# First attention of a two-layer transformer kernel: value products by a table of chunks, maxima of two banks taken at once, no repeated products

## What is computed

```python
q = layer_norm(qkv[:, :, 0], q_gamma, q_beta)
k = layer_norm(qkv[:, :, 1], k_gamma, k_beta)
v = qkv[:, :, 2]
q, k = apply_rope(q, k)
attn = jnp.einsum('bqhd,bkhd->bhqk', q * D ** -0.5, k)      # 16 heads of 16
attn = jax.nn.softmax(attn, axis=-1)
out = jnp.einsum('bhqk,bkhd->bqhd', attn, v).reshape(B, S, C)
out = jnp.einsum('bsc,oc->bso', out, w_proj) + b_proj
```

## Time and profile before

| | |
|---|---|
| median of three runs | 1911.12 us (1906.89 to 1915.96) |
| the profiled execution | 1908.63 us, of it 1906.6 us span of instructions |
| first maximum take of the first attention | 133.0 us from the span's start |
| last transpose of maxima (L867) | 767.9 us |
| last maximum take (L1000) | 764.4 us |
| granted PE clock over the span | 0.968 of full speed |

### The profile page before, as it was taken

The page is one execution under the profiler, slowest core; times in us unless marked ns, Lnnn a source line. Parts: engine busy times, 40 slices in busy tenths (PEclk is TensorE's granted clock), DMA queues, the critical chain, the costliest instruction groups (busy, mean ns, idle before and its releaser), DMA issues. The chain is left out here.

```text
span 1906.6 us, 34780 instructions
## 1 busy us (share of the span) xinstructions
PE 1798.0 (94%) x12778; PEld 1176.0 (62%) x12778; DVE 1430.6 (75%) x2814; ACT 1116.5 (59%) x2212; POOL 529.8 (28%) x686
## 2 busy tenths in 40 slices
PE   8989999999999999799999989999999987999995
PEld 4545444444444444388888875555555566999994
DVE  7879999999999999367677656567666454766665
ACT  4645888888888888622333215455463632655555
POOL 5760000233000001032223212212425243544444
PEclk9976999999999999899999999999999998999998
DMA  4883734565434512023444256545565324565555
GB/s 170 279 261 50 127 74 101 128 145 124 87 57 70 80 33 86 18 78 111 153 143 148 89 189 139 142 99 145 145 155 152 111 78 152 151 152 144 144 114 199
DMA packets 146599, 239.18 MB, mean 125 GB/s; under 512 B 25829, under 2 KB 81158, under 8 KB 146448
## 3 DMA queue, kind: packets, MB, share of 16 engines
q1 hardware_dynamic: 113312, 171.48, 36.7%
q0 software_dynamic: 17024, 34.25, 7.0%
q10 hardware_dynamic: 16112, 31.46, 4.5%
HBM read 137.49 MB, written 96.60 MB: 123 GB/s over the span
## 5 line engine op out<-in xcount | busy, mean ns | idle before, releaser
L1000 DVE TENSOR_REDUCE b_mx<-b_PM 128x1 f32<-128x512 f32 x1024 | 621.3, 682 | 18.5 <-PE b_PM L854 18.1
L976 ACT ACTIVATE b_probs<-b_PS 128x512 f32<-128x512 f32 x1000 | 524.1, 607 | 69.2 <-PE b_PS L908 53.6
L854 PE MATMUL b_PM<-b_kst,b_qst 48*128 48x512 f32 x888 | 281.8, 431 | 0.0
L2929 ACT ACTIVATE d_probs<-d_PS 128x512 f32<-128x512 f32 (+3 forms) x384 | 166.0, 497 | 183.4 <-PE d_PS L2830 167.5
L908 PE MATMUL b_PS<-b_qst,b_kst 50*128 50x512 f32 x744 | 257.2, 437 | 1.8
L2968 DVE TENSOR_REDUCE d_mx<-d_PM 128x2 f32<-128x1024 f32 (+1 forms) x192 | 179.5, 950 | 92.4 <-PE d_PM L2782 50.8
L908 PEld LDWEIGHTS b_PS<-b_qst,b_kst 50*128 50x128 f32 x744 | 120.4, 184 | 163.6 <-ACT b_probs L976 148.1
L2884 POOL TENSOR_SCALAR_AFFINE_SELECT d_probs<-d_probs 128x128 f32<-128x128 f32 x256 | 74.1, 303 | 265.6 <-ACT d_probs L2929 260.7
L796 POOL CAST b_mhalves<-b_maxima 128x16 fp32r<-128x16 f32 x32 | 6.3, 196 | 506.8 <-DVE b_maxima L1009 506.8
L854 PEld LDWEIGHTS b_PM<-b_kst,b_qst 48*128 48x128 f32 x888 | 142.1, 185 | 5.3
L880 PE MATMUL b_PO<-b_probs,x_v 128*32 128x384 f32 (+2 forms) x2048 | 145.2, 390 | 0.0
(11 more groups left out here) (322 smaller groups left out, 3751.2 us busy)
## 6 DMA issues: line engine op xcount, KB each, us to landing
halves<-a_parts SPq DMA_DIRECT2D x7, 2048.0 KB, 8.7
qk<-c_halves ACTq DMA_DIRECT2D x7, 2048.0 KB
w_w<-L_ffn_fc1T SPq DMA_DIRECT2D x12, 1024.0 KB, 5.0
w_w<-L_ffn_fc2T SPq DMA_DIRECT2D x12, 1024.0 KB
b_qst<-halves SPq DMA_DIRECT2D x72, 128.0 KB, 4.3
b_kst<-halves SPq DMA_DIRECT2D x72, 128.0 KB, 7.2
d_qst<-qk SPq DMA_DIRECT2D x36, 256.0 KB, 5.1
d_kst<-qk SPq DMA_DIRECT2D x36, 256.0 KB, 7.3
```

Source lines behind the costliest of these rows:

```text
L854: mm = pe.matmul(PM[n % MBANKS][:], qst[buf][at, p, first:first + P], kst[buf][at, p, kh * BLK:(kh + 1) * BLK], start=True, stop=True)
L976: act.activation(probs[:, s % RING], score_bank(g, s)[:], ACT.Exp).then_inc(exped, 1)
L1000: dve.tensor_reduce(mx[:, half, (r * PAIRS0 + p) * TPH + t, kh:kh + 1], PM[n % MBANKS][:], AX.X, ALU.max)\
L2929: act.activation(probs[:, s % RING, 0:w], PS[bank(s)][:, 0:w], ACT.Exp).then_inc(exped, 1)
```

## The change

- `REPEATS` is emptied: each maximum product is issued once.
- The bursts are gone. After each unit PE issues the value products that the table `CHUNKS` names for it: an entry is (unit of the half after whose products it comes, round, first quarter, end quarter). An entry of 32 or more falls in the next half. An entry covers one round, and there are 13 per half in 12 places. The transpose stays behind the units 22 and 54.
- The output is copied after the units 41 and 9 (before: 36 and 4).
- `PM` becomes one tensor of four banks, and `mx` is set to -3e38 once. For the steps in `WHOLE_STEPS`, 12 of 32 in a group, and all 24 steps that are made ahead of the first group, the DVE waits for both products, takes the maximum over both banks (1024 elements) in one instruction, and raises `max_taken` by 2 when it is done. The second column of `mx` keeps -3e38 there.
- In the last group, the rounds from unit 23 on begin with one round more of values.

```diff
-    LAG, BREAK = 6, 3
-    REPEATS = {7: 3, 8: 2, 9: 2, 10: 2}
...
+    REPEATS = {}
+
+    CHUNKS = [(12, 0, 0, 3), (15, 0, 3, 4), (16, 1, 0, 3), (19, 1, 3, 4), (19, 2, 0, 2), (22, 2, 2, 4),
+              (25, 3, 0, 2), (27, 3, 2, 4), (30, 4, 0, 4), (33, 5, 0, 4), (36, 6, 0, 2), (38, 6, 2, 4),
+              (41, 7, 0, 4)]
+
+    def values_after(s):
+
+        found = []
+        for half in range(HALVES):
+            for at, R, first, end in CHUNKS:
+                at += half * UNITS // HALVES
+                if at % UNITS == s:
+                    found.append((-(at // UNITS), half * TPB + R, first, end))
+        return sorted(found)
...
+    COPY_UNITS = [41, 9]
+    WHOLE_STEPS = [2, 4, 6, 11, 13, 15, 18, 20, 22, 27, 29, 31]
+
+    def whole(n):
+
+        n -= AHEAD * HALVES
+        return n < 0 or n % UNITS // HALVES in WHOLE_STEPS
...
-        PM = [a.ps(f"PM{i}", [P, BLK]) for i in range(MBANKS)]
+        PM = a.ps("PM", [P, MBANKS, BLK])
...
-            def burst(g, k):
-                for s in units_of(k):
-                    score(g, s)
-                for i, at in enumerate(TURN_PLACES):
-                    u = HALVES * g + 1 + i
-                    if at // SBANKS == k and u < TURNS:
-
-                        pe.wait_ge(exped, g * UNITS + exps_before(at - SBANKS + 1) + SBANKS)
-                        turn_max(u)
-                for before, R, first, end in values_after(k):
+            def unit(g, s):
+                score(g, s)
+                if s + 1 in TURN_UNITS and (u := HALVES * g + 1 + TURN_UNITS.index(s + 1)) < TURNS:
+
+                    pe.wait_ge(exped, g * UNITS + exps_before(TURN_PLACES[TURN_UNITS.index(s + 1)] - SBANKS + 1) + SBANKS)
+                    turn_max(u)
+                for before, R, first, end in values_after(s):
                     if g + before >= 0:
                         values(g + before, R, first, end)
...
-            s, v = WIDE_FROM, quarters_through(WIDE_BURST - 1)
-            for R in range(WIDE_FROM // G0 + 1, ROUNDS + 2):
+            s, v = WIDE_FROM, quarters_until(WIDE_FROM)
+            for R in range(v // G0 + 2, ROUNDS + 2):
...
+            dve.memset(mx[:], -3.0e38).then_inc(mx_set, 1)
+            dve.wait_ge(mx_set, 1)
...
-                dve.wait_ge(max_scores, n + 1)
-                dve.tensor_reduce(mx[:, half, (r * PAIRS0 + p) * TPH + t, kh:kh + 1], PM[n % MBANKS][:], AX.X, ALU.max)\
-                   .then_inc(max_taken, 1)
+                out = mx[:, half, (r * PAIRS0 + p) * TPH + t]
+                if not whole(n):
+                    dve.wait_ge(max_scores, n + 1)
+                    dve.tensor_reduce(out[:, kh:kh + 1], PM[:, n % MBANKS], AX.X, ALU.max).then_inc(max_taken, 1)
+                elif kh == 0:
+                    dve.wait_ge(max_scores, n + HALVES)
+                    both = PM[:, n % MBANKS:n % MBANKS + HALVES].rearrange("p h n -> p (h n)")
+                    dve.tensor_reduce(out[:, 0:1], both, AX.X, ALU.max).then_inc(max_taken, HALVES)
```

More of the change, by code:

```diff
@@ L630, in exps_before, with quarters_until @@
         return sum(place(s) < at for s in range(UNITS)) - sum(place(s) - LAPS >= at for s in range(UNITS))
-    LAG, BREAK = 6, 3
-    REPEATS = {7: 3, 8: 2, 9: 2, 10: 2}
-    def quarters_through(k):
-        last = units_of(k)[-1] if k >= 0 else -1
-        def due(v):
-            w = v % (UNITS // HALVES)
-            return last >= v + LAG + max(0, BREAK - w // G0)
-        return sum(due(v) for v in range(-UNITS, UNITS)) - UNITS
-    def values_after(k):
-        v, end, found = quarters_through(k - 1), quarters_through(k), []
-        while v < end:
-            stop = min(end, v // G0 * G0 + G0)
-            found.append((v // UNITS, v % UNITS // G0, v % G0, (stop - 1) % G0 + 1))
-            v = stop
-        return found
-    def copied_after(half):
-        end = UNITS // HALVES if half == 0 else 0
-        k = min(k for k in range(BURSTS) if quarters_through(k) >= end)
-        return units_of(k)[-1] - 1
-    COPY_UNITS = [copied_after(half) for half in range(HALVES)]
+    REPEATS = {}
[10 more added lines that the diff above has]
+        return sorted(found)
+    def quarters_until(s):
+        return sum(end - first for half in range(HALVES) for at, R, first, end in CHUNKS if at + half * UNITS // HALVES < s)
+    assert all(at >= R * G0 + G0 - 1 for at, R, first, end in CHUNKS)
+    COPY_UNITS = [41, 9]
[3 more added lines that the diff above has]
+        return n < 0 or n % UNITS // HALVES in WHOLE_STEPS
     def step_at(x):
@@ L853, in max_product @@
                 for _ in range(times):
-                    mm = pe.matmul(PM[n % MBANKS][:], qst[buf][at, p, first:first + P],
+                    mm = pe.matmul(PM[:, n % MBANKS], qst[buf][at, p, first:first + P],
                                    kst[buf][at, p, kh * BLK:(kh + 1) * BLK], start=True, stop=True)
@@ L938, in _ @@
             for g in range(GROUPS):
-                for k in range(BURSTS if g < GROUPS - 1 else WIDE_BURST):
-                    burst(g, k)
-            s, v = WIDE_FROM, quarters_through(WIDE_BURST - 1)
-            for R in range(WIDE_FROM // G0 + 1, ROUNDS + 2):
+                for s in range(UNITS if g < GROUPS - 1 else WIDE_FROM):
+                    unit(g, s)
+            s, v = WIDE_FROM, quarters_until(WIDE_FROM)
+            for R in range(v // G0 + 2, ROUNDS + 2):
                 while s < min((R + 1) * G0, UNITS):
```

15 lines of the change are left out of this document (6 added, 9 removed).

## The result

Four runs of the changed kernel took 1971.77 us in the median (1967.34 to 1976.85), the kernel before beside them 1910.03 (1906.89 to 1915.96): a ratio of **1.0333** (95% interval 1.0306 to 1.0361), 61.7 us more. The forecast was 1949, the range ended at 1964. One remark for all comparisons: layer 1, which no kernel here changes, differs by up to 18 us between profiled executions, so that small differences are read within the attention.

A forecast was written before the change was run, and what follows sets the result against it. The DVE was taken to bound the first attention, PE just behind. Terms: +0.4 and +38.3 from +1.32 a half over 29 halves, +2.0 lead, -1.5 cold start: +39 on 1908.63, forecast 1949 us, range 1925 to 1964.

The forecast's parts named there:

- 12/13 to 22/23: Stretch of a half between the merged takes of these units: 6.47 us forecast, of which 0.46 DVE idle.
- Two products behind one wait. This decides: Merged takes await both products, free banks together; work between three pairs per half idles the DVE: +1.32 us a half.
- pairs 20, 21, 22 and the transpose: Step of PE's work before merged take 22/23, costed at 0.34 + 0.24 + 1.16 us.
- ACT doesn't interfere: ACT's exps and copies in a half need about 17 of 21 us, so they were taken not to delay anything.
- 0.57 from product 13 to its take: Delay from the second product of split pair 12/13 to the merged take's start; also used at 22/23 and 30/31.
- 12 x 0.17 = +2.0: Lead of 24 merged steps at half clock: 2.56 us per merged pair against 2.39 single; bounds -1.3 and +4.
- I take -1.5: Group 0's cold start: fewer repeated products and quarters before the clock rises save 1.5 us; bounds -4 and +2.
- The last group's rest is paced by exps and stays: End of the attention, rest of the last group: no change in time, forecast 0.
- They cover idle time, so I cost their removal at nothing: Five repeated products per half, units 7 to 10: they fill PE's idle time, so removing them costs nothing at full clock.
- Rival 1: Faster: DVE has 0.33 us less a half, no new waits; half 18.90 us, whole 1886 us; chance 8%.
- Rival 2: Slower by less: only two direct stops count; half 20.3 us, whole 1929 us; chance 12%.
- rival 3: Clock falls without the repeated products: one slow stretch every four groups adds some 15 us, 1964 us; chance 5%.

The follow-up runs named there:

- e1: Changed kernel with every take single, in the lead too; table and single products stay: 19.25 us a half, median 1905.39 us, ratio 0.9963.
- e6: Table of chunks with single takes, lead included, plus merged takes at units 24/25 and 28/29 of each half: 19.15 us a half, 1902.46 us, ratio 0.9944.
- e7: Table of chunks with single takes, lead included, plus merged takes at 12/13 and 30/31, split by values: 20.06 us a half, 1926.92 us, ratio 1.0075.
- e9: Changed kernel with the values of units 22 and 54 issued before the transpose, not behind it: 21.22 us a half, 1965.29 us, ratio 1.0267.
- e13 to e16: One chip, in order: changed kernel again 1969.13 us; it with single lead 1980.59; table with single takes but merged lead 1905.55; table alone again 1903.91.
- e8: Table with single takes, merges at 24/25 and 28/29, last group's first output copied after unit 36 instead of 41: 19.15 us a half, 1899.32 us, ratio 0.9923.
- e10: Table with single takes, lead included, and the repeated products back in units 7 to 10 of each half: 19.64 us a half, 1919.34 us, ratio 1.0029.
- e12: Kernel before with only the repeated products removed; bursts and single takes stay: 20.09 us a half, 1926.70 us, ratio 1.0083.
- e16: Second run of the table with all takes single, lead included, and no repeated products: 1903.91 us.
- e4: Kernel before with the merged takes alone, lead included; bursts, repeats and output copies as before: 20.76 us a half, 1948.92 us, ratio 1.0178.

## Why the prediction was right and wrong

The forecast was 23 us too low. The mechanism, two products behind one wait, held; what failed are the size of one of its pieces (12/13 to 22/23), the cold start and the last group.

- **The bound and the rhythm: right.** The DVE set the pace and PE was just behind. Its need of 19.23 us a half is what e1 takes, with no idle time at all.
- **"Two products behind one wait. This decides": right in kind, and within 0.08 us in four of five pieces.** All four are at or above the forecast. From 8/9 to 12/13 I had 3.04 (3.12 in the timeline above), 26/27 to 30/31 3.26 (3.32), 22/23 to 26/27 2.34 (2.34), 30/31 to 8/9 5.87 (mean of the halves 5.87). e6 and e7 show the cause by itself, for the pairs that values split.
- **The piece from 12/13 to 22/23 failed: 6.47 forecast, 6.88 in the timeline.** By its own steps: product 16 came 0.14, not 0.05, after the take (525.20 against 523.83 + 1.23); the transpose came 0.29 later than the step "pairs 20, 21, 22 and the transpose" had it; the way from product to merged take was 0.64, not 0.57. The middle one is the largest. I took the transpose's 1.16 from the earlier trace rows, where three scores stand in a burst whose exps are long done. In the table unit 22 comes 0.24 behind unit 21, and the transpose writes into a `PS` bank that waits for an exp. "ACT doesn't interfere" compared sums (17 of 21 us), and the wait is one of order. e9 takes it away and gives back 0.27.
- **"0.57 from product 13 to its take" was mis-sized:** 0.63 at all three split pairs. The 0.57 of the earlier trace rows is a take of one bank, and e7, where 22/23 isn't merged, still has it there (0.57) beside 0.63 at its two merged pairs. Three times 0.06 are 0.2 a half. Why a take of two banks starts 0.06 later was not tried.
- Together these make 0.5 us a half: 21.49 instead of 20.98, and over 28 halves 14.6 of the 25 us between the 39 of the sum and the 64 that the last exp came later. The rest is 1.2 in the lead, 4.3 to take 22, 2.4 in the next piece and 2.4 at the end.
- **"12 x 0.17 = +2.0" for the lead: 3.2 measured,** inside its bounds.
- **"I take -1.5" for the cold start: the wrong sign.** To take 22 of group 0 it is +2.8, and the next piece is 2.4 more than forecast. I counted what PE has less to do before the clock rises and took the moment of the rise as given; it came later (granted clock 0.52 from 160 to 192 us, against 0.77 before). Only partly explained, see e13 to e16.
- **"The last group's rest is paced by exps and stays": wrong by 2.4.** I didn't follow `COPY_UNITS` into the last group, where the order of exps, not the DVE, decides when `PO` is free: 1.3 us of pause, and 1.2 by the clock that fell with it (e8).
- **"They cover idle time, so I cost their removal at nothing": wrong in both directions.** In the table the repeats would have cost 0.39 a half (e10); in the bursts they hold up the clock (e12, +0.8%). In this change as a whole these don't show, since the table keeps the clock without them.
- **The saving of 0.055 per merge: right** (0.06 in e6). The Trainium skill ("VectorE: DVE Perf Modes", the cycle table of the TRN2 errata section) has 120 fixed cycles for an operation on PSUM, 0.125 us at 0.96 GHz. e6 shows half of that, since consecutive takes overlap by 0.08 us. The Trainium skill's rule to minimize the number of chained operations ("VectorE: DVE Perf Modes", Rules for kernel authors) holds in e6, where the inputs are there, and is turned round in e7, where they are not.
- **Rival 1 (1886 us)** was excluded by the split pairs. Rival 2 (20.3 a half) was too low, rival 3 wrong for this kernel (1.00 between 230 and 800 us) and right for e12.
- **The range** held bounds for the unknown costs only. (Its sum is also off by one: 1947.8 and 2.5 make 1950, not 1949. And the +7 for "no saving by merging" would be 9.6 by its own 0.33 a half over 29 halves.) The steady half, priced step by step from single rows, had none above, and each 0.1 us that is missed in it counts 29 times.

## What to carry to other kernels

Where an engine is 99% busy, first ask in what order its inputs come. Joining two of its operations ties both inputs and both buffers together: the producer gets its buffers back later and in pairs, and whatever stands between the two inputs is waited for. A merge was worth 0.06 us where its inputs lay ready and cost about 0.4 us or more where something stood between them. When a half of a loop is priced from single rows, take each step from a place with the same neighbours, and give the sum an error that grows with the number of repetitions. A change of order must be followed into the first and the last round, where other engines set the pace.

## What the hardware showed that I had not expected

- **The clock fell in the steady bursts of e12** though PE's longest idle time there was 0.55 us: 0.98 over 560 us, and from 189 to 756 us nine stretches of about 3.4 us at 1.2 GHz, behind an idle 0.54 us and four pairs 0.49 us apart. The same pause stands in every half, but the clock fell in only nine, all of them second halves of a group. The same kernel with five more products a half in that place held 1.00, and so did e1 with neither repeats nor bursts.
- **The end of the cold start varies** from 172 to 196 us over the 18 executions, and by up to 9 us between two of the same kernel (e1 and e16), though PE was idle for no more than 0.2 us between its first score and the rise.
- **After an idle of 2.54 us at the end of the attention** the clock fell as well: 1.93 us for values that had taken 1.06. It did so in ten of the 14 executions with this pause and not in the other four; behind the 0.97 us that PE stands idle there in the kernel before, e4 and e12 it never fell.
